# LSTM over gathered gate rows: each node tile's rows stay in a place of their own, and a gather fetches only the rows whose index changed

## The chip, the cores and the metric

The kernel runs on one core of a Trainium2 chip. The metric is the device time of one execution in microseconds; the median of several runs counts. The core has a matrix engine (TensorE, PE), a vector engine (VectorE, DVE), an activation engine (ScalarE, ACT), a general engine (GpSimd, POOL), a queue processor (SyncE, SP) and 16 DMA engines. Engines run their own instruction streams and wait for each other through semaphores.

## The reference

A graph of 6250 nodes has 106250 edges (50000 random ones in both directions, and a loop for each node), sorted by the receiver `dst`. Two layers run one after the other, each added to its input and normalised. The first is an LSTM over 17 neighbours of each node, where the "neighbours" are read from `dst`:

```python
col = edge_index[1]                       # = dst, which is sorted
seq = x[col].reshape(n, 17, 128)
# for each of the 17 steps, over all 6250 nodes:
gates = x_t @ w_ih.T + h @ w_hh.T + b     # 512 columns
i, f, g, o = split(gates, 4)
c = sigmoid(f) * c + sigmoid(i) * tanh(g)
h = sigmoid(o) * tanh(c)
x = layernorm(x + h_last @ w_lin.T + b_lin)
```

The second is an edge stage: for each edge a small MLP over 8 features gives weights, they are multiplied with 4 edge attributes and with the sender's row (gathered by `src`), and the messages are summed by `dst`, projected, added and normalised.

## The kernel before

Nodes stand in 49 tiles of 128 (6272 places, 22 of them padding), and the tiles in 13 chunks: 12 of 512 nodes and a last, narrow one of 128. The input part of the gates, x @ w_ih.T, depends on the node that is read and not on the step, so it is computed once for each node (`table_tile`, L330) and stored to the table `gates` in HBM, 2 KB a row. Step 0 gathers rows of x itself instead (L306), turns and multiplies them (`first_turn`, `first_gates`), so that it needn't wait for the table. Steps 1 to 16 are the list `WORK`, 208 pairs (step, chunk), in which index k counts.

For each k:

- POOL issues one indirect DMA for each of the chunk's tiles (L318). It takes 128 indices, a column of `seq_index`, and brings 128 rows of 2 KB from `gates`, one into each partition. They go to one of SLOTS = 5 slots (`rows[:, k % SLOTS]`); from the sixth on POOL first waits until the chunk 5 places back has been turned (`s_turned`, L314). Each gather has a semaphore of its slot, `s_wait[k % SLOTS]`.
- PE waits for the rows (L420). `turn_gate(k, q)` transposes the rows of gate q into a PSUM bank, 4 transposes for each gate and full chunk (L386), and `from_hidden(k, q)` adds the product with the hidden state, three matmuls of 512 columns, since weights and state are split in a high and a low part (L396). The order is turn 0, 1, 2, from_hidden 0, 1, 2, turn 3, from_hidden 3. Banks 0 to 3 belong to even k, 4 to 7 to odd k, so turn 0 waits for the DVE product two chunks back, turn 2 for the cell, turn 3 for `h_lo` (`s_hidden`).
- ACT applies sigmoid or tanh to the four gates (L562) and tanh to the cell of the chunk before (L529).
- DVE makes i*g (L728), the hidden product of the chunk before (L690), its high part (L695), f*c (L733), the low part (L700) and the sum (L738): six operations for each chunk. Nine further operations over 832 columns (`besides`, L648 to L682) prepare the edge stage, one behind each chunk from step 2 on.

SP loads the weights of the edge stage, x^T into `x1` and the attributes, 26 loads, one behind every second chunk from the start of WORK (L283 to L285). A factor is applied to a part of `w_out` on DVE in step 8 (L741). Behind the last step DVE's `residual(0)` (L783), the linear layer, the normalisation and the table of senders form a bridge (L436 to L800); POOL clears the sums in it (L325). The edge stage works in half groups of 4 edge tiles. POOL gathers 128 senders of 512 bytes for each tile (L862, 832 gathers), up to 4 half groups ahead of DVE's messages (L1040). ACT scales (L984), DVE multiplies (L1029 to L1040), PE runs the MLP (L877, L884, L896) and sums by receiver (L928).

SBUF holds `shared` (cell, the 5 slots and two candidates), beside `x1`, `attr`, `src_index` and others at places of their own.

Of the kernel before, what the change touches and what calls it, by code (L numbers as in the profile page):

```python
# [9 lines left out]
F32 = mybir.dt.float32  # L10
F32R = mybir.dt.float32r
I32 = mybir.dt.int32
# [26 lines left out]


# [16 lines left out]
RING = 4  # L57

# [40 lines left out]
def build(nc, t):  # L99
    ctx = ExitStack()  # L100
    with ctx:
# [10 lines left out]
        x1 = sb("x1", [P, NODE_TILES, DIM])  # L112
        dst = sb("dst", [P, EDGE_TILES])
        rel = sb("rel", [P, EDGE_TILES])
        base_row = sb("base_row", [P, EDGE_TILES])
        base_turn = sb("base_turn", [P, EDGE_TILES])
        iota = sb("iota", [P, P])
        src_index = sb("src_index", [P, EDGE_TILES], I32)
        attr = sb("attr", [P, 4, EDGE_TILES])
        ones = sb("ones", [P, 1])  # L120
        ident = sb("ident", [P, P])
        eps = sb("eps", [P, 1])
        w_up = sb("w_up", [P, P])
        a1 = sb("a1", [P, GROUP * P])
        a2 = sb("a2", [P, P])
        a3 = sb("a3", [P, P])
        b12 = sb("b12", [P, 2])
        w_out = sb("w_out", [P, MSG])
        w_lin = sb("w_lin", [P, P])
        b_lin = sb("b_lin", [P, 1])  # L130
        rounds_word = sb("rounds_word", [1, 1], I32)
        stats = sb("stats", [P, NODE_TILES, 6])
        moments = sb("moments", [P, NODE_TILES, 2])
        rstd = sb("rstd", [P, NODE_TILES])
        moments1 = sb("moments1", [P, NODE_TILES, 2])
        rstd1 = sb("rstd1", [P, NODE_TILES])


        slot_cols = 4 * 4 * HID
        pool_cols = SLOTS * slot_cols + 2 * CHUNK  # L140
        shared = sb("shared", [P, NODE_COLS + pool_cols])
        acc = shared[:, 0:NODE_TILES * MSG].rearrange("p (n f) -> p n f", f=MSG)
# [3 lines left out]
        s_wait = [sem(f"s_gather{i}") for i in range(SLOTS)]  # L146

        def flat_view(tile):
            return tile[:].rearrange("p a n -> p (a n)")

        def flat(tile, slot):
            return tile[:, slot].rearrange("p a n -> p (a n)")

        with ExitStack() as scope:

            cell = shared[:, 0:NODE_COLS]
            pool_of = shared[:, NODE_COLS:NODE_COLS + pool_cols]
            rows = pool_of[:, 0:SLOTS * slot_cols].rearrange("p (s j n) -> p s j n", s=SLOTS, j=4)
            candidate = pool_of[:, SLOTS * slot_cols:pool_cols].rearrange("p (s n) -> p s n", s=2)

            x_t = cell
            in_rows = pool_of[:, 0:8 * CHUNK].rearrange("p (s n) -> p s n", s=8)
            w_ih = pool_of[:, 8 * CHUNK:9 * CHUNK]

            seq_index = sb("seq_index", [P, NODE_TILES * STEPS], I32, scope=scope)
            not_below = sb("not_below", [P, EDGE_TILES], scope=scope)
            dst_int = not_below[:].bitcast(I32)
            mean_of = not_below[:, 0:P]
            count = sb("count", [P, 1], scope=scope)
            missed = sb("missed", [1, 1], scope=scope)  # L170
            bias2 = sb("bias2", [P, 8], scope=scope)
# [10 lines left out]
            up = sb("up", [P, 2, 4, P], scope=scope)  # L182
            inside = up[:].rearrange("p s j d -> p (s j d)")[:, 0:EDGE_TILES]

            s_wts, s_seq, s_idx, s_rest = sem("s_wts"), sem("s_seq"), sem("s_idx"), sem("s_rest")
            s_xt = [sem(f"s_xt{i}") for i in range(5)]
# [58 lines left out]

            def rows_in(c):
                return slice(FOURS[c][0], FOURS[c][-1] + 1)
# [10 lines left out]
            with nc.Block() as block:  # L258
                @block.sync
                def _(sp):  # L260
# [4 lines left out]
                    for tile, name in ((ident[:], "ident"), (bias2[:], "bias2"), (w_hh, "w_hh"), (w_lin[:], "w_lin")):  # L265
                        sp.dma_start(tile, t[name]).then_inc(s_idx, 16)
                    for n in range(NODE_TILES):
# [5 lines left out]
                    sp.dma_start(base_row[:], t["base_row"]).then_inc(s_const, 16)  # L273
                    sp.dma_start(base_turn[:], t["base_turn"]).then_inc(s_const, 16)
                    small = [(tile[:], t[name]) for tile, name in (
                        (src_index, "src"), (w_up, "w_up"), (a1, "a1"), (a2, "a2"),
                        (a3, "a3"), (b12, "b12"), (w_out, "w_out"), (b_lin, "b_lin"), (iota, "iota"))]
                    large = [(x1[:, tiles[0]:tiles[-1] + 1, :].rearrange("p a d -> p (a d)"),
                              t["x_t"][:, tiles[0] * P:(tiles[-1] + 1) * P]) for tiles in FOURS]
                    large += [(attr[:, k, :], t["attr4"][:, k * EDGE_TILES:(k + 1) * EDGE_TILES]) for k in range(4)]  # L280
                    loads = small + large
# [13 lines left out]
                def _(pool):  # L295
                    pool.memset(ones[:], 1.0)
                    pool.memset(eps[:], 1e-5).then_inc(s_set, 1)
                    pool.wait_ge(s_set, 1)
                    pool.wait_ge(s_seq, 16)
                    for c, (c0, width) in enumerate(CHUNKS):  # L300
# [4 lines left out]
                        for n in range(c0 // P, (c0 + width) // P):  # L305
                            pool.indirect_dma_start(  # L306
                                out=x1[:, n, :], out_offset=None, in_=t["x_rows"],
                                in_offset=bass.IndirectOffsetOnAxis(ap=seq_index[:, n * STEPS:n * STEPS + 1], axis=0),
                            ).then_inc(z_rows[c % SLOTS], 16)
# [15 lines left out]
                    pool.memset(shared[:, 0:NODE_TILES * MSG], 0.0).then_inc(s_zero, 1)  # L325
# [3 lines left out]
                def _(pe):  # L329
# [11 lines left out]
                    def first_turn(c):  # L341
# [11 lines left out]
                        for j in range(width // P):  # L353
                            last = pe.transpose(x_bank(c)[:, j * P:(j + 1) * P], x1[:, c0 // P + j, :], ident[:])
# [17 lines left out]
                    def turn_gate(k, q):  # L372
# [12 lines left out]
                        for j in range(CHUNKS[c][1] // P):  # L385
                            last = pe.matmul(bank[:, j * P:(j + 1) * P], rows[:, k % SLOTS, j, cols], ident[:],  # L386
# [25 lines left out]
                    landed = [0] * SLOTS  # L412
                    for k, (step, c) in enumerate(WORK):
                        c0, width = CHUNKS[c]
                        landed[k % SLOTS] += 16 * (width // P)
# [4 lines left out]
                        pe.wait_ge(s_wait[k % SLOTS], landed[k % SLOTS])  # L420
# [825 lines left out]
```

## Time and profile before

| | |
|---|---|
| median of 3 runs | 2174.67 us (2174.66 to 2175.22) |
| span of the profiled execution | 2710.9 us |
| PE, DVE, ACT, POOL busy in that span | 79%, 59%, 55%, 58% |
| granted TensorE clock, mean | 0.875 of full speed |
| moved by DMA | 299.97 MB, of it 263.36 MB by the software queue (the gathers) |

The page gives the span of the profiled execution, from its first to its last instruction, and no time for what lies around it. The span is 536 us longer than the median of the runs without a profile. Durations of single instructions are read from it; lengths of stages include what the profile adds. Times of instructions and idle times are in us, means of one instruction in ns. A releaser called "issue" means that nothing the profile shows held the engine back, "remote" that the releaser isn't known. Ends of matmuls are modelled. PE's clock has two levels, 1.2 and 2.4 GHz; the granted clock is the share of the upper one.

### The profile page before, as it was taken

What the parts mean: (1) busy time and instruction counts of PE and PEld (TensorE: products, weight loads), DVE (VectorE), ACT (ScalarE), POOL (GpSimd) and SP (SyncE); (2) the same over time, 40 slices, a digit from 0 to 9 for tenths busy, and PEclk for the clock granted to TensorE, in tenths of its full rate; (3) what the DMA queues carried; (4) which work ended last, traced back from release to release, by engine and by line L of the source; (5) the groups of instructions that cost most, each with busy time, mean ns of one, the idle gap of its engine ahead of it and who ended that gap; (6) DMA issues with size and microseconds to landing.
All of it is one profiled execution on the core that took longest, in us unless ns stands there. A gap on an engine that the chain in (4) does not pass through costs nothing.

```text
span 2710.9 us, 32629 instructions
## 1 busy us (share of the span) xinstructions
PE 2142.9 (79%) x10173; PEld 1641.3 (61%) x10173; DVE 1597.6 (59%) x3607; ACT 1490.2 (55%) x4706; POOL 1585.6 (58%) x1673
## 2 busy tenths in 40 slices
PE   6688888888888888888777777777778777877776
PEld 4567666776777767677555555555555555555554
DVE  4567566656666666666645545555555555555555
ACT  4545455445555555555366655656566656665655
POOL 5466666666666666665355555555556655655553
PEclk8899899899999999998778888778877888888888
DMA  6566666665665666565211111111111111112111
GB/s 236 170 195 183 193 206 188 181 173 171 178 180 170 181 173 180 170 178 152 67 40 46 45 41 44 43 41 45 45 39 47 46 41 46 47 40 75 41 42 41
DMA packets 118698, 299.97 MB, mean 111 GB/s; under 512 B 29058, under 2 KB 42604, under 8 KB 118524
## 3 DMA queue, kind: packets, MB, share of 16 engines
q0 software_dynamic: 90912, 263.36, 34.7%
q1 hardware_dynamic: 27612, 34.51, 3.8%
q8 instruction: 82, 1.34, 0.2%
q14 instruction: 92, 0.75, 0.1%
HBM read 278.50 MB, written 19.26 MB: 110 GB/s over the span
## 4 chain that ended last, share of the span: by engine, by line
ACT 21%; another core or an unknown queue 13%; PE 9%; issue 7%; DVE 1%; ACTq 0%; DVEq 0%
ACT bank L984 20%; PE bank L928 4%; PE bank L896 2%; PE bank L877 1%; PE bank L884 1%; ACT h L972 0%; ACT h L964 0%; PE bank L907 0%; PE bank L908 0%; DVE side L1029 0%; DVE msg L1032 0%; DVE msg L1030 0%; DVE y_high L1072 0%; PE bank L903 0%
## 5 line engine op out<-in xcount | busy, mean ns | idle before, releaser
L862 POOL DMA_INDIRECT sender<-table,src_index x832 | 784.8, 943 | 585.9 <-DVE msg L1040 303.3
L318 POOL DMA_INDIRECT shared<-gates,seq_index x784 | 742.1, 947 | 447.0 <-issue 207.6
L984 ACT ACTIVATE bank<-bank,attr 128x64 f32<-128x64 f32 x3328 | 702.2, 373 | 1.1 <-PE bank L896 0.5
L562 ACT ACTIVATE bank<-bank,bias 128x512 f32<-128x512 f32 (+1 forms) x624 | 375.7, 633 | 452.8 <-PE bank L396 329.2
L386 PE MATMUL bank<-ident,shared 128*128 128x128 f32 x3136 | 466.1, 292 | 173.3 <-DVE h_lo L700 135.0
L386 PEld LDWEIGHTS bank<-ident,shared 128*128 128x128 f32 x3136 | 396.9, 151 | 260.2 <-DVE h_lo L700 166.1
L928 PE MATMUL bank<-msg,select 128*128 128x256 f32 x1664 | 512.1, 453 | 1.2 <-DVE msg L1040 1.2
L1029 DVE TENSOR_TENSOR side<-sender,bank 128x192 f32<-128x192 f32 x416 | 146.6, 352 | 553.0 <-ACT bank L984 401.4
L896 PEld LDWEIGHTS bank<-a,h 64*128 64x128 f32 x1664 | 239.3, 219 | 349.6 <-issue 222.7
L896 PE MATMUL bank<-a,h 64*128 64x128 f32 x1664 | 282.6, 319 | 156.6 <-ACT bank L984 111.9
L928 PEld LDWEIGHTS bank<-msg,select 128*128 128x128 f32 x1664 | 349.0, 224 | 74.9 <-issue 7.4
L396 PE MATMUL bank<-h_hi,w_lo 128*128 128x512 f32 (+1 forms) x832 | 369.0, 443 | 1.1 <-issue 1.1
L728 DVE TENSOR_TENSOR shared<-bank,shared 128x512 f32<-128x512 f32 (+1 forms) x208 | 136.6, 657 | 393.6 <-ACT shared L562 205.8
L396 PE MATMUL bank<-h_hi,w_hi 128*128 128x512 f32 (+1 forms) x832 | 333.0, 400 | 0.0
L396 PE MATMUL bank<-h_lo,w_hi 128*128 128x512 f32 (+1 forms) x832 | 332.6, 400 | 0.3 <-issue 0.3
L964 ACT ACTIVATE h<-bank,b 128x512 f32<-128x512 f32 x104 | 74.1, 713 | 277.3 <-remote 185.0
L972 ACT ACTIVATE h<-bank,b 128x512 f32<-128x512 f32 x104 | 74.6, 717 | 256.5 <-remote 170.6
L877 PE MATMUL bank<-feats,a 128*128 128x512 f32 x208 | 128.8, 705 | 87.0 <-ACT h L972 60.8
L884 PE MATMUL bank<-h,a 128*128 128x512 f32 x208 | 130.0, 711 | 84.8 <-ACT h L964 78.1
L396 PEld LDWEIGHTS bank<-h_hi,w_hi 128*128 128x128 f32 x832 | 166.2, 200 | 34.7
L396 PEld LDWEIGHTS bank<-h_hi,w_lo 128*128 128x128 f32 x832 | 169.4, 204 | 19.6 <-issue 1.5
L396 PEld LDWEIGHTS bank<-h_lo,w_hi 128*128 128x128 f32 x832 | 168.7, 203 | 19.3 <-issue 1.3
(119 smaller groups left out, 2389.8 us busy)
## 6 DMA issues: line engine op xcount, KB each, us to landing
sender<-table,src_index POOLq DMA_INDIRECT x832
gates<-shared SPq DMA_DIRECT2D x49, 256.0 KB
shared<-gates,seq_index POOLq DMA_INDIRECT x784
feats<-attr_in SPq DMA_DIRECT2D x13, 256.0 KB
x<-x_t_in SPq DMA_DIRECT2D x12, 256.0 KB
table<-up SPq DMA_DIRECT2D x12, 256.0 KB, 2.3
out<-shared SPq DMA_DIRECT2D x9, 256.0 KB
shared<-x_t_in SPq DMA_DIRECT2D x3, 704.0 KB, 9.8
```

Source lines behind the costliest of these rows:

```text
L318: pool.indirect_dma_start(out=rows[:, k % SLOTS, j, :], out_offset=None, in_=t["gates"], in_offset=bass.IndirectOffsetOnAxis(ap=seq_index[ ...
L386: last = pe.matmul(bank[:, j * P:(j + 1) * P], rows[:, k % SLOTS, j, cols], ident[:], is_transpose=True, start=(j == 0), stop=False, skip_ ...
L396: last = pe.matmul(bank[:, 0:width], w[:, cols], h[:, c0:c0 + width], start=False, stop=(w is w_hi and h is h_hi), skip_group_check=True)
L562: act_e.activation(candidate[:, k % 2, 0:width] if gate == 2 else values, values, ACT.Tanh if gate == 2 else ACT.Sigmoid, bias=bias2[:, ga ...
L728: dve.tensor_tensor(added, put, added, ALU.mult).then_inc(s_ig, 1)
L862: pool.indirect_dma_start(out=sender[:, hg % 4, j, :], out_offset=None, in_=t["table"], in_offset=bass.IndirectOffsetOnAxis(ap=src_index[: ...
L877: pe.matmul(mlp_bank[:], a1[:, b * P:(b + 1) * P], feats[:, s % 2, :], start=True, stop=True).then_inc(e_p1, 1)
L884: pe.matmul(mlp_bank[:], a2[:], h1[:, g % 2, :], start=True, stop=True).then_inc(e_p2, 1)
L896: last = pe.matmul(weight_bank[hg % 2][:, j * P:(j + 1) * P], h2[channels, g % 2, j * P:(j + 1) * P], a3[channels, :], start=True, stop=True)
L928: last = pe.matmul(acc_bank[i % 2][:, 0:MSG], select[:, hg % RING, j, :], msg[:, hg % RING, j].rearrange("p k u -> p (k u)"), start=(tile ...
L984: last = act_e.activation(wy[:, j, :, k, :], w[:, 2 * i + j, :, min(k, 1), :], ACT.Copy, scale=attr[:, k, tile:tile + 1])
L1029: dve.tensor_tensor(along, row[:, :, 1:4, :], wy[:, :, 1, 1:4, :], ALU.mult).then_inc(e_side, 1)
```

## The change

All large buffers move into one SBUF tensor, `arena`, and share places over time. `rows` now has a place for each of the 49 node tiles (49 x 512 columns), which takes the room of `x1`, `attr`, `src_index`, `a1` to `a3`, `w_out`, `iota` and `acc` during the LSTM. A gather for (step, chunk) writes over the same tile's rows of the step before, so for step 2 and on it waits until that chunk was turned in the step before (13 places back), and in step 1 the last chunks wait until step 0's gates are done. Each chunk has a semaphore of its own.

At the start DVE makes a list `fetch` from `seq_index`: where a node's index of step t equals that of step t - 1 (t from 2 on), 65536 is added. The gathers use this list with a bound of 6271 and without an error beyond it, so a row with a larger index isn't fetched, and the place keeps the row of the step before. Step 0 and step 1 fetch all rows.

Since `x1` and the others now lie under `rows`, 23 of SP's loads move into the last step, each behind the transposes that free its place, and DVE scales `w_out` just ahead of `residual(0)`. `base_row` and `base_turn` share one buffer, so the second is loaded once the first has been used. The arithmetic is the same.

```diff
+SKIP = 1 << 16
...
+            rows = part(ROWS, NODE_TILES * ROW).rearrange("p (n g) -> p n g", g=ROW)
...
+            def last_row_end(end):
+                return before_last + ((end - ROWS - 1) // ROW) // 4 + 1
...
-                    for i, (tile, source) in enumerate(loads):
-                        sp.wait_ge(s_act, 8 * (i + 1))
+                    for tile, end, source in late:
+                        sp.wait_ge(s_turned, last_row_end(end))
                         sp.dma_start(tile, source).then_inc(s_rest, 16)
...
-                    pool.wait_ge(s_seq, 16)
+                    pool.memset(seq_same, 0.0).then_inc(s_fetch, 1)
+                    pool.wait_ge(s_fetch, 4)
...
                     for k, (step, c) in enumerate(WORK):
-                        if k >= SLOTS:
-                            pool.wait_ge(s_turned, k - SLOTS + 1)
                         c0, width = CHUNKS[c]
-                        for j in range(width // P):
-                            col = (c0 // P + j) * STEPS + step
+                        if step > 1:
+                            pool.wait_ge(s_turned, k - NCH + 1)
+                        elif ROWS + (c0 + width) // P * ROW > W_LIN:
+                            pool.wait_ge(z_gate, 3 * NCH)
+                        for n in range(c0 // P, (c0 + width) // P):
+                            col = n * STEPS + step
                             pool.indirect_dma_start(
-                                out=rows[:, k % SLOTS, j, :], out_offset=None, in_=t["gates"],
-                                in_offset=bass.IndirectOffsetOnAxis(ap=seq_index[:, col:col + 1], axis=0),
-                            ).then_inc(s_wait[k % SLOTS], 16)
+                                out=rows[:, n, :], out_offset=None, in_=t["gates"],
+                                in_offset=bass.IndirectOffsetOnAxis(ap=fetch[:, col:col + 1], axis=0),
+                                bounds_check=NODE_COLS - 1, oob_is_err=False,
+                            ).then_inc(s_wait[c], 16)
...
-                        pe.wait_ge(s_wait[k % SLOTS], landed[k % SLOTS])
+                        pe.wait_ge(s_wait[c], 16 * (width // P) * step)
...
+                    dve.wait_ge(s_seq, 16)
+                    dve.tensor_copy(seq_number, seq_index).then_inc(s_fetch, 1)
+                    dve.wait_ge(s_fetch, 2)
+                    dve.tensor_tensor(later, numbers[:, :, 2:STEPS], numbers[:, :, 1:STEPS - 1],
+                                      ALU.is_equal).then_inc(s_fetch, 1)
+                    dve.wait_ge(s_fetch, 3)
+                    dve.scalar_tensor_tensor(fetch[:], seq_same, float(SKIP), seq_number, ALU.mult,
+                                             ALU.add).then_inc(s_fetch, 1)
...
+                    scale_out()
                     residual(0)
```

## Rows read from the trace of the kernel before

**Rows 1.** Busy time of each engine by stretch; clock, DMA share and GB/s last
```profile
core 0: us, PE busy (x) PEld busy (x) DVE busy (x) ACT busy (x) POOL busy (x), PEclk, DMA share, GB/s
0.00:91.00 91.00, 62.37 (x252) 46.73 (x252) 47.81 (x71) 43.39 (x69) 48.01 (x55) 0.92 0.65 224
...
124.00:1296.00 1172.00, 997.24 (x5634) 838.21 (x5634) 756.75 (x1258) 599.58 (x1039) 723.37 (x765) 0.93 0.62 178
...
1339.00:2683.00 1344.00, 1022.08 (x3962) 706.57 (x3963) 723.46 (x2037) 809.97 (x3499) 784.79 (x832) 0.83 0.18 45
```
**Rows 2.** Groups by line, POOL: count, busy us, mean ns, idle before and releasers
```profile
L862 POOL DMA_INDIRECT sender<-table,src_index x832 | 784.8, 943 | 585.9 <-DVE msg L1040 303.3 <-issue 282.6
L318 POOL DMA_INDIRECT shared<-gates,seq_index x784 | 742.1, 947 | 447.0 <-issue 207.6 <-remote 152.6 <-PE bank L386 80.4
L306 POOL DMA_INDIRECT x<-x_rows_in,seq_index x49 | 47.7, 973 | 36.7 <-PE bank L337 20.6 <-issue 12.2 <-DMA seq_index<-seq_index_in 3.9
```
**Rows 3.** Timeline, POOL: start us, us, line; idle time before in brackets
```profile
91.59 0.94 POOL L318 DMA_INDIRECT shared<-gates,seq_index  x1 [6.31 <-DMA gates<-shared]
92.83 0.95 POOL L318 DMA_INDIRECT shared<-gates,seq_index  x1 [0.30 <-issue]
94.08 0.95 POOL L318 DMA_INDIRECT shared<-gates,seq_index  x1 [0.30 <-issue]
...
130.75 0.95 POOL L318 DMA_INDIRECT shared<-gates,seq_index  x1 [14.46 <-PE bank L386]
...
208.64 1.09 POOL L318 DMA_INDIRECT shared<-gates,seq_index  x1 [0.30 <-issue]
```
**Rows 4.** Timeline of PE, ACT and DVE, 697 to 710 us
```profile
697.06 1.47 PE L386 MATMUL bank<-ident,shared 128*128 128x128 f32 x12
...
698.84 0.40 PE L396 MATMUL bank<-h_hi,w_hi 128*128 128x512 f32 x1
...
701.60 1.47 PE L386 MATMUL bank<-ident,shared 128*128 128x128 f32 x12
...
703.60 0.66 ACT L562 ACTIVATE bank<-bank,bias 128x512 f32<-128x512 f32 x1 [5.67 <-remote]
...
705.51 0.69 DVE L690 TENSOR_TENSOR bank<-bank,tanh_c 128x512 f32<-128x512 f32 x1
...
708.17 0.66 PE L386 MATMUL bank<-ident,shared 128*128 128x128 f32 x4 [3.03 <-DVE h_lo L700]
...
709.42 0.70 DVE L690 TENSOR_TENSOR bank<-bank,tanh_c 128x512 f32<-128x512 f32 x1
```
**Rows 5.** Timeline: PE's last LSTM matmul, POOL's first and last edge gather
```profile
1295.73 0.28 PE L396 MATMUL bank<-h_hi,w_hi 128*128 128x128 f32 x1
...
1339.29 0.95 POOL L862 DMA_INDIRECT sender<-table,src_index  x1 [27.20 <-issue]
...
2681.82 0.94 POOL L862 DMA_INDIRECT sender<-table,src_index  x1 [0.30 <-issue]
```
**Rows 6.** Timeline of PE in the narrow chunk of the last step
```profile
1293.98 0.28 PE L396 MATMUL bank<-h_hi,w_lo 128*128 128x128 f32 x1
1294.09 0.28 PE L396 MATMUL bank<-h_lo,w_hi 128*128 128x128 f32 x1
1294.20 0.28 PE L396 MATMUL bank<-h_hi,w_hi 128*128 128x128 f32 x1
1295.39 0.33 PE L386 MATMUL bank<-ident,shared 128*128 128x128 f32 x1 [0.92 <-DVE h_lo L700]
```
**Rows 7.** Timeline of PE and ACT from the end of step 0 into step 1
```profile
97.06 0.50 PE L368 MATMUL bank<-first_hi,w_lo 128*128 128x512 f32 x1 [1.33 <-DVE h_lo L623]
...
104.96 0.60 ACT L513 ACTIVATE first_hi<-bank 128x512 fp32r<-128x512 f32 x1 [2.58 <-PE bank L354]
...
106.33 0.50 PE L368 MATMUL bank<-first_hi,w_lo 128*128 128x512 f32 x1 [2.72 <-issue]
...
121.99 0.47 PE L368 MATMUL bank<-first_hi,w_lo 128*128 128x128 f32 x1 [13.29 <-DVE first_lo L623]
...
123.97 2.78 PE L386 MATMUL bank<-ident,shared 128*128 128x128 f32 x12
```
**Rows 8.** Groups by line and shape, DVE operations over 832 columns
```profile
L654 DVE TENSOR_TENSOR rel<-dst,base_row 128x832 f32<-128x832 f32 x1 | 1.0, 1040 | 0.0
L662 DVE SCALAR_TENSOR_TENSOR up<-rel,not_below 128x832 f32<-128x832 f32 x1 | 1.0, 1017 | 0.0
...
L650 DVE CAST dst<-not_below 128x832 f32<-128x832 int32 x1 | 0.6, 583 | 0.0
```
**Rows 9.** DMA queues (packets, MB, share) and issues (KB each, us to landing)
```profile
q0 software_dynamic: 90912, 263.36, 34.7%
...
table<-up SPq DMA_DIRECT2D x12, 256.0 KB, 2.3
```

More of the change, by code:

```diff
@@ L38 @@
 SLOTS = 5
+SKIP = 1 << 16
+ROW = 4 * HID
+CELL = 0
+ROWS = CELL + NODE_COLS
+CAND = ROWS + NODE_TILES * ROW
+ARENA = CAND + 2 * CHUNK
+IN_ROWS = ROWS
+W_IH = IN_ROWS + 8 * ROW
+INDEX = W_IH + ROW
+X_ROWS = CAND - NODE_COLS
+W_LIN = X_ROWS - P
 GROUP = 8
@@ L57 @@
 RING = 4
+Y_LOW = 0
+X1 = ROWS
+ATTR = X1 + NODE_COLS
+SRC = ATTR + 4 * EDGE_TILES
+A1 = SRC + EDGE_TILES
+A2 = A1 + GROUP * P
+A3 = A2 + P
+W_OUT = A3 + P
+IOTA = W_OUT + MSG
+ACC = IOTA + P
+STATS = ACC + NODE_TILES * MSG
+MOMENTS = STATS + 6 * NODE_TILES
+RSTD = MOMENTS + 2 * NODE_TILES
+MOMENTS1 = Y_LOW + 36 * DIM
+RSTD1 = MOMENTS1 + 2 * NODE_TILES
+assert RSTD1 + NODE_TILES <= X1 and RSTD + NODE_TILES <= CAND
 def window_starts():
@@ L109, in sem, with part @@
             return ctx.enter_context(nc.semaphore(name))
-        x1 = sb("x1", [P, NODE_TILES, DIM])
+        arena = sb("arena", [P, ARENA])
+        def part(start, cols):
+            return arena[:, start:start + cols]
+        x1 = part(X1, NODE_COLS).rearrange("p (n d) -> p n d", d=DIM)
+        attr = part(ATTR, 4 * EDGE_TILES).rearrange("p (k n) -> p k n", k=4)
+        src_index = part(SRC, EDGE_TILES).bitcast(I32)
+        a1, a2, a3 = part(A1, GROUP * P), part(A2, P), part(A3, P)
+        w_out, iota = part(W_OUT, MSG), part(IOTA, P)
@@ L136, in build @@
[L136 to L142, printed above, removed]
+        rounds_word = small[0:1, 5:6].bitcast(I32)
         banks = [ps(f"bank{i}", [P, 512]) for i in range(8)]
         s_const = sem("s_const")
-        s_wait = [sem(f"s_gather{i}") for i in range(SLOTS)]
-        def flat_view(tile):
-            return tile[:].rearrange("p a n -> p (a n)")
@@ L151, in flat @@
-        def flat(tile, slot):
-            return tile[:, slot].rearrange("p a n -> p (a n)")
+        s_wait = [sem(f"s_gather{i}") for i in range(NCH)]
         with ExitStack() as scope:
[L156 to L159, printed above, removed]
+            cell = part(CELL, NODE_COLS)
+            rows = part(ROWS, NODE_TILES * ROW).rearrange("p (n g) -> p n g", g=ROW)
+            candidate = part(CAND, 2 * CHUNK).rearrange("p (s n) -> p s n", s=2)
@@ L385, in turn_gate @@
                         for j in range(CHUNKS[c][1] // P):
-                            last = pe.matmul(bank[:, j * P:(j + 1) * P], rows[:, k % SLOTS, j, cols], ident[:],
+                            last = pe.matmul(bank[:, j * P:(j + 1) * P], rows[:, CHUNKS[c][0] // P + j, cols], ident[:],
                                              is_transpose=True, start=(j == 0), stop=False,
@@ L484, in _ @@
                     pe.matmul(banks[5][:, P:2 * P], mean_of, w_up[:], start=True, stop=True)
-                    pe.matmul(banks[5][0:1, 0:1], count[:], ones[:], start=True, stop=True).then_inc(s_count, 1)
+                    pe.matmul(banks[5][0:1, 0:1], count, ones, start=True, stop=True).then_inc(s_count, 1)
                     for c in range(groups):
@@ L740, in _ @@
                             besides.pop(0)()
-                        if step == STEPS // 2 and c == 0:
-                            view = w_out[3 * MUL:P, P:2 * P]
-                            dve.wait_ge(s_rest, rest)
-                            dve.tensor_scalar(view, view, float(1 / np.sqrt(np.float32(3))), None, ALU.mult)
                     hidden_product(len(WORK) - 1)
@@ L781, in scale_projected, with scale_out @@
                             ALU.mult, ALU.mult).then_inc(s_up, 1)
+                    def scale_out():
+                        view = w_out[3 * MUL:P, P:2 * P]
+                        dve.wait_ge(s_rest, rest)
+                        dve.tensor_scalar(view, view, float(1 / np.sqrt(np.float32(3))), None, ALU.mult)
+                    scale_out()
                     residual(0)
@@ L883, in mlp2 @@
                         pe.wait_ge(e_h1, g + 1)
-                        pe.matmul(mlp_bank[:], a2[:], h1[:, g % 2, :], start=True, stop=True).then_inc(e_p2, 1)
+                        pe.matmul(mlp_bank[:], a2, h1[:, g % 2, :], start=True, stop=True).then_inc(e_p2, 1)
                     def mlp3(hg):
```

140 lines of the change are left out of this document (71 added, 69 removed).

## The prediction, made before the changed kernel was built or run

> **What bounds the kernel now.** I read the totals of the stages first, then the groups of the GpSimd queue (POOL), then single stretches in order of time. The span has two long stages: the LSTM steps 1 to 16 (124 to 1296 us) and the edge stage (1339 to 2683 us) [rows 1]. In the first, TensorE (PE) is busy 997 of 1172 us, VectorE (DVE) 757, ScalarE (ACT) 600, and the DMA engines 62%. None is full. POOL's busy time is little but the issuing of gathers: 784 gathers for the LSTM, 832 for the edges, 49 for step 0, about 945 ns each [rows 2]. Behind each comes a gap of 0.30 us that no other engine ends, so they start 1.25 us apart [rows 3]. That is 784 x 1.25 = 980 us in the LSTM and 832 x 1.25 = 1040 us in the edge stage, whatever the row size: a 512-byte row and a 2048-byte row cost the same 943 and 947 ns [rows 2].
>
> The profiled span is 2710.9 us, the median of the runs 2174.67 us; the page gives nothing of what lies around the span, so 536 us exist only under the profile. The trace shows where: from about 105 us on, ACT stands still every 12 us or so with its input ready. PE has finished the first gate's matmuls of a chunk at 699.2 us, ACT takes them at 703.60 after 5.67 us of idleness with an unknown releaser, and DVE and PE queue behind it (PE stops 3.03 us until h_lo is written at 708.1) [rows 4]. The first such hole ends at 104.96 us [rows 7]. So I don't take the stage lengths of the profile, but rebuild an undisturbed run from its durations.
>
> Ledger for an undisturbed run, POOL leading: first LSTM gather 91.6 us [rows 3]; + 980 = 1071.6; PE behind the last gathers + 7.3 (2.3 for a 256 KB transfer to land, as the table's store shows [rows 9], + 4.54 + 1.75 for the last two chunks, below, - 1.25 as the last full chunk's rows are issued one gather earlier) = 1079; to the first edge gather 43.3 (1296.0 to 1339.3) [rows 5]; + 1040; + 28.2 from POOL's last gather to the end (2682.8 to 2711) [rows 5]. Sum 2190, 16 us over the measured 2174.67. That closes within 0.7% with no free number, so I read the kernel as bound by POOL's issue rate in both stages.
>
> Ledger with PE leading in the LSTM: a full chunk of 512 nodes without a wait takes 4.54 us (transposes of one chunk at 697.06, of the next at 701.60) [rows 4]. A narrow chunk of 128 nodes takes 12 matmuls at 0.112 us and 4 transposes at about 0.1 us, 1.75 us; behind it PE waits 0.92 us for h_lo, and I put 0.75 us to it [rows 6]. A step is 12 x 4.54 + 1.75 + 0.75 = 57.0 us, 16 steps are 912 us. PE starts step 1 at 123.97 us, behind holes of 13.29 and 2.72 us caused by ACT, of which DVE's own chain would need some 1.3 [rows 7]; undisturbed that is about 109.3 us. So PE could be done at 109.3 + 912 = 1021 us, and the total would be 2132 us, 43 us under the measured time. The first ledger is the nearer.
>
> **The change, part by part.**
> - Rows fetched. dst is sorted and a node's 17 indices are consecutive, so almost all of a node's steps have the same index. Counted from the inputs, 5,522 of the 94,080 rows of steps 2 to 16 change, 7.5 of 128 in a gather; step 1 fetches all. The instructions stay 784. What falls for certain are bytes of the software queue's 263 MB [rows 9]: 784 x 256 KB, 205 MB, become some 24 MB. They are worth nothing by themselves: the DMA engines are at 62% [rows 1].
> - POOL's price of a gather. No row shows a gather with fewer rows. From below: if the 945 ns go with the rows fetched, 7.5/128 of them, 0.06 us, and the gap of 0.30 remain, 0.36 us. From above: the slowest LSTM gather in the stretch I read took 1.09 us, 0.14 more, so 1.39 us with the gap [rows 3]. The 128 indices must still be read and compared. I take a price nearer the lower end, since for 94% of the rows no transfer has to be made up. The exact value doesn't matter: POOL ends before PE as soon as 91.6 + 784 p + 7.3 is under 1021, at p below 1.176 us, 8% off the 945 ns. Then PE leads, and the stage ends at 1021 instead of 1079: **-58 us**.
> - The rule of the Trainium skill that bears on this: DMA: Bandwidth & Descriptors, section SWDGE vs HWDGE vs iDMA, says that software on the GpSimd cores computes one descriptor pair for each DMA operation. By that rule the price follows the rows not skipped, 0.36 us, and the total is the same 2117 us, with PE leading by far. By the trace (no dependence on bytes) the price could as well be one of the instruction, and the total 2174 us. The rows here can't decide between these.
> - A place for each node tile instead of a ring of 5 chunks. A gather of step t waits for the transposes of its own chunk in step t-1, 13 chunks back instead of 5. In the profile POOL stands 14.46 us at 116 us for the first slot (its row of 130.75) [rows 3], but undisturbed PE would have turned that chunk at about 115 us, so I count 0 (if the hole were real, 14 us of gain). It also lets POOL run ahead of ACT's holes, which helps the profile alone.
> - Start. POOL and DVE first make the list: a cast of 833 columns 0.58, a compare 1.04, a multiply-add 1.02 us, by the same operations on 832 columns [rows 8]. DVE's w_hi begins some 2 us after 4.54 and low(0) is ready at 7.7 instead of 7.64. The cover is ACT's h_hi, which is on the path anyway. POOL's first step-0 gather moves by 2.7 us; it waits for PE later. 0 us; without the cover 2.7.
> - Loads moved into the last step: 23 of them, 6.2 MB, each after the transposes that free its place; the last place is free once chunk 5 of 13 is turned, 25 us into the step, so 32 us remain. At the 224 GB/s of the first stretch [rows 1] all 6.2 MB take 28 us, and most begin earlier. Hidden, 0 us. Behind them are queued DVE's scaling of w_out and then residual(0), and PE's mean matmul, so if they are late the bridge moves by the lateness, up to about 5 us. The scaling itself adds one 128-column operation, 0.3 us at most.
> - Whether DVE and ACT keep up with PE: DVE's product comes every 3.91 us when it is not waiting (705.51 to 709.42) [rows 4], under 4.54. It is next, with 14% to spare.
>
> Sum: 2174.67 - 58 = **2117 us**. Against the profiled span the same edit is worth less or more, depending on what becomes of ACT's holes; I forecast only the runs.
>
> **The rivals.**
> 1. The price stays. If the 945 ns belong to the instruction (all 128 indices read and compared, vectors of fixed length), POOL leads as before and only the byte count falls: 2174 us, 2168 to 2179. The same results if the change doesn't do what it says (the rows beyond the bound are fetched from somewhere), or if the missing 43 us of the second ledger lie in the edge stage and PE already leads the LSTM. For it: equal times for both row sizes. Against: the ledger that closes.
> 2. The price rises: slower. With a bound given, each gather may carry another register instruction, or take a slower loop. POOL is the bound, so all 784 pay in full; from +0.006 us each it is over 0.2%. Between 0 and the +0.14 us above I take +0.05: 784 x 0.05 = 39, 2214 us. Against it: 94% of the rows leave work out.
> 3. Only part: a price between 1.176 and 1.24 us, or PE meets waits I don't see (narrow chunks, h_lo) and loses 5 to 40 us of the 58: 2125 to 2165 us.
>
> **How the numbers follow.** Forecast 0.52 (2117; own range 2095 to 2135: PE's wait at the narrow chunk 0 to 1.5 us a step is +-12, the two ledgers' distance of 16 and 43 us lets the gain be 43 to 74). Rival 1: 0.22, of which 0.17 within 0.2%. Rival 2: 0.20. Rival 3: 0.06. Faster 0.52 + 0.06 + 0.05 = 0.63, same 0.17, slower 0.20; 0.2% (4.3 us) is about what a measurement of this kernel can tell from no change. The range runs from 2095 over rival 3 and rival 1 to 2200, and leaves out most of rival 2 and a little below.
>
> **What would show it.** In the profile after: the start-to-start time of the LSTM gathers in steps 2 to 16, well under 1.176 us for the forecast, 1.25 for rival 1, above for rival 2; in step 1, with all rows fetched, 1.25 or more. POOL should wait for PE's transposes through the whole LSTM, PE should have no wait that ends with a landing, and its clock should stay at the upper level. The software queue's 263 MB should fall to some 82 MB. The last loads should land before the last chunk. Edge gathers unchanged at 1.25 us. The prediction fails if the compare costs as much as a descriptor, or if PE doesn't reach 4.54 us a chunk in undisturbed runs.

## The result, and the profile after

The changed kernel takes 2212.76 us (median of 4 runs, 2212.12 to 2214.28), the kernel before 2174.66 us (4 runs, 2171.55 to 2175.22): ratio 1.018, 95% interval 1.0168 to 1.0193, 38.1 us slower. The forecast was 2117 us, faster. What came is rival 2, whose sum was 2214 us.

One thing must be known to read the traces. The profiled execution of the changed kernel spans 2211.7 us in a run of 2213.39 us, and the other three runs took 2212.12 to 2214.28 us, so a profile adds nothing. The profile of before (2710.9 us) looks like the profiles of four chips met below, on which the median of the kernel before was 2700 to 2775 us and the profiled run was no longer than the rest (e1: 2694.33 us among runs of 2682.09 to 2727.99). I read it as taken on such a chip; its chip isn't on record. I call a chip "plain" if the kernel before takes about 2175 us there, and "halting" if it takes 2700 to 2775 us. A ratio is always against runs of the kernel before on the same chip.

The page of the changed kernel: its span, its DMA packets, the software queue (packets, MB, share of 16 engines), and the shares of the chain that ended last by engine.

```profile
span 2211.7 us, 33416 instructions
...
DMA packets 118704, 119.01 MB, mean 54 GB/s; under 512 B 70886, under 2 KB 84432, under 8 KB 118524
...
q0 software_dynamic: 90912, 82.35, 15.5%
...
POOL 35%; issue 11%; PE 1%; DVE 0%; DMA 0%; ACT 0%; POOLq 0%; SPq 0%; DVEq 0%
```

The page before has, for all queues together:

```profile
DMA packets 118698, 299.97 MB, mean 111 GB/s; under 512 B 29058, under 2 KB 42604, under 8 KB 118524
```

The bytes fell as planned, from 263.36 to 82.35 MB, but the queue's packet count is the same 90912 as before [rows 9]: skipped rows still leave their packets, small ones (70886 are now under 512 bytes, 29058 were before). The chain that ended last is POOL's edge gathers and the gaps behind them; it begins at 1150 us, behind the LSTM, so of the LSTM it says nothing; there POOL's idle time has to. POOL's groups of the changed kernel, times busy and idle in us, mean in ns:

```profile
L908 POOL DMA_INDIRECT sender<-table,arena x832 | 785.3, 944 | 280.8 <-issue 279.3 <-DVE msg L1086 1.5
L351 POOL DMA_INDIRECT arena<-gates,fetch x784 | 785.2, 1001 | 244.6 <-issue 233.3 <-DMA gates<-arena 5.9 <-PE bank L420 5.5
L337 POOL DMA_INDIRECT arena<-x_rows_in,fetch x49 | 48.6, 992 | 20.6 <-issue 12.8 <-DVE fetch L744 5.0 <-PE bank L371 2.5
```

Against [rows 2], the edge gathers, which weren't changed, kept their price (943 and 944 ns); the LSTM gathers went from 947 to 1001 ns. POOL waits 5.5 us for PE's transposes in all, and not through the whole LSTM. Gathers of the changed kernel one by one, in step 1, where every row is fetched, and in the middle of the stage, where 7.5 of 128 are (start, duration, what ended the idle time before):

```profile
79.41 1.00 POOL L351 DMA_INDIRECT arena<-gates,fetch  x1 [0.31 <-issue]
80.71 0.99 POOL L351 DMA_INDIRECT arena<-gates,fetch  x1 [0.30 <-issue]
82.01 1.00 POOL L351 DMA_INDIRECT arena<-gates,fetch  x1 [0.30 <-issue]
...
707.58 1.00 POOL L351 DMA_INDIRECT arena<-gates,fetch  x1 [0.31 <-issue]
708.89 1.00 POOL L351 DMA_INDIRECT arena<-gates,fetch  x1 [0.30 <-issue]
710.19 1.00 POOL L351 DMA_INDIRECT arena<-gates,fetch  x1 [0.30 <-issue]
```

They start 1.303 us apart in both places, where [rows 3] had 1.25: a gather with the bound is the longer one even where it skips nothing. 784 x 0.052 is 41 us, and the result is +38.1. The groups of PE's waits (total us, times, longest), the weight loads of the same transposes, which run ahead of them, and the busy time of the LSTM show who is late:

```profile
PE bank L420 <- DMA arena<-gates,fetch: 63.3, 131, 1.3
PE bank L420 <- DVE h_lo L733: 15.0, 16, 0.9
```

```profile
L420 PEld LDWEIGHTS bank<-ident,arena 128*128 128x128 f32 x3136 | 355.0, 141 | 174.1 <-DMA arena<-gates,fetch 125.2
```

```profile
core 0: us, PE busy (x) PEld busy (x) DVE busy (x) ACT busy (x) POOL busy (x), PEclk, DMA share, GB/s
110.00:1103.00 993.00, 915.00 (x5544) 755.47 (x5543) 743.90 (x1237) 604.65 (x1021) 759.80 (x760) 1.00 0.12 26
```

PE waits for landings 131 times (63.3 us; its weight loads 125.2 us), and the DMA engines are busy 12% of the stage: what PE waits for are gathers not yet issued, not rows on their way. The granted clock is 1.00 here, PE's upper level, so the clock cost nothing.

### The profile page after: what moved, and what is told of

The parts are those of the page before. It is cut to its first block and busy times, and to the rows that moved or that the text cites. A ratio compares the mean times of both kernels' runs of the same rounds, so it can differ in the third digit from the quotient of the medians.

```text
span 2211.7 us, 33416 instructions
## 1 busy us (share of the span) xinstructions
PE 1911.1 (86%) x10173; PEld 1475.6 (67%) x10173; DVE 1582.1 (72%) x3610; ACT 1513.0 (68%) x4706; POOL 1631.0 (74%) x1674
## 2 busy tenths in 40 slices
DMA packets 118704, 119.01 MB, mean 54 GB/s; under 512 B 70886, under 2 KB 84432, under 8 KB 118524
## 3 DMA queue, kind: packets, MB, share of 16 engines
q0 software_dynamic: 90912, 82.35, 15.5%
## 5 line engine op out<-in xcount | busy, mean ns | idle before, releaser
L908 POOL DMA_INDIRECT sender<-table,arena x832 | 785.3, 944 | 280.8 <-issue 279.3
L351 POOL DMA_INDIRECT arena<-gates,fetch x784 | 785.2, 1001 | 244.6 <-issue 233.3
L1030 ACT ACTIVATE bank<-bank,arena 128x64 f32<-128x64 f32 x3328 | 697.3, 337 | 178.6 <-DVE msg L1078 175.7
L594 ACT ACTIVATE bank<-bank,small 128x512 f32<-128x512 f32 (+1 forms) x624 | 393.6, 634 | 366.4 <-PE bank L430 355.8
L420 PE MATMUL bank<-ident,arena 128*128 128x128 f32 x3136 | 419.5, 275 | 78.9 <-DMA arena<-gates,fetch 63.3
L420 PEld LDWEIGHTS bank<-ident,arena 128*128 128x128 f32 x3136 | 355.0, 141 | 174.1 <-DMA arena<-gates,fetch 125.2
L942 PEld LDWEIGHTS bank<-arena,h 64*128 64x128 f32 x1664 | 205.1, 191 | 335.1 <-issue 183.2
L942 PE MATMUL bank<-arena,h 64*128 64x128 f32 x1664 | 242.8, 287 | 163.5 <-ACT bank L1030 162.0
L1076 DVE TENSOR_TENSOR msg<-sender,bank 128x256 f32<-128x256 f32 x416 | 171.5, 412 | 0.0
L1078 DVE TENSOR_TENSOR msg<-sender,bank 128x192 f32<-128x192 f32 x416 | 143.7, 345 | 0.0
```

Of the source, the lines that this page charges most:

```text
L351: pool.indirect_dma_start(out=rows[:, n, :], out_offset=None, in_=t["gates"], in_offset=bass.IndirectOffsetOnAxis(ap=fetch[:, col:col + 1] ...
L420: last = pe.matmul(bank[:, j * P:(j + 1) * P], rows[:, CHUNKS[c][0] // P + j, cols], ident[:], is_transpose=True, start=(j == 0), stop=Fal ...
L594: act_e.activation(candidate[:, k % 2, 0:width] if gate == 2 else values, values, ACT.Tanh if gate == 2 else ACT.Sigmoid, bias=bias2[:, ga ...
L908: pool.indirect_dma_start(out=sender[:, hg % 4, j, :], out_offset=None, in_=t["table"], in_offset=bass.IndirectOffsetOnAxis(ap=src_index[: ...
L942: last = pe.matmul(weight_bank[hg % 2][:, j * P:(j + 1) * P], h2[channels, g % 2, j * P:(j + 1) * P], a3[channels, :], start=True, stop=True)
L1030: last = act_e.activation(wy[:, j, :, k, :], w[:, 2 * i + j, :, min(k, 1), :], ACT.Copy, scale=attr[:, k, tile:tile + 1])
```

## The experiments

My theory after the result: the bound itself makes a gather's instruction 0.05 us longer, whatever it skips. The rivals: the list of skipped rows costs (time per row compared or skipped); the writes into a large arena cost; the extra instruction of each bounded gather costs.

**Bound and skipping apart.** e1 takes the bound away and fetches all rows into the places:

```diff
-                                bounds_check=NODE_COLS - 1, oob_is_err=False,
...
-                    dve.scalar_tensor_tensor(fetch[:], seq_same, float(SKIP), seq_number, ALU.mult,
+                    dve.scalar_tensor_tensor(fetch[:], seq_same, 0.0, seq_number, ALU.mult,
```

> The changed kernel with the bound and the list's additions taken out: places for all tiles stay, every gather fetches all 128 rows (263 MB again). Theory B (the bound given with the instruction adds 52 ns to each LSTM gather, and POOL's queue sets the time): LSTM gathers 945 ns, 1.25 us apart, total 2213 - 784 x 0.052 = 2172 us. Rival P (the price comes from the new places or from the index list's place): 1.30 us apart, 2213 us. Rival S (the skipping costs): 2172 us as well.

e2 has only the second of these edits: the bound stands, and no index is beyond it.

> The changed kernel with the bound kept, but no index ever beyond it: all rows are fetched, 263 MB. Theory B: gathers 1000 ns, 1.30 us apart, 2213 us, so the 181 MB that the change saves are worth nothing. Rival S (rows that are skipped cost more than rows that are fetched): 945 ns, 2172 us. A rival in which skipping already gives something back: above 1000 ns and above 2213 us.

e3 is the kernel before with the bound:

```diff
                                 in_offset=bass.IndirectOffsetOnAxis(ap=seq_index[:, col:col + 1], axis=0),
+                                bounds_check=NODE_COLS - 1, oob_is_err=False,
```

> The kernel before, ring of 5 slots, with nothing but the bound given to its LSTM gathers; no index lies beyond it. Theory B: 2175 + 784 x 0.052 = 2215 us. Rivals P and S: 2175 us, no change.

e7 puts all indices from step 2 on beyond the bound, so the steps compute with the rows of step 1:

```diff
-                    pool.memset(seq_same, 0.0).then_inc(s_fetch, 1)
+                    pool.memset(seq_same, 1.0).then_inc(s_fetch, 1)
...
-                    dve.tensor_tensor(later, numbers[:, :, 2:STEPS], numbers[:, :, 1:STEPS - 1],
-                                      ALU.is_equal).then_inc(s_fetch, 1)
+                    dve.tensor_scalar(seq_same.rearrange("p (n t) -> p n t", t=STEPS)[:, :, 0:2],
+                                      numbers[:, :, 0:2], 0.0, None, ALU.mult).then_inc(s_fetch, 1)
```

> The changed kernel with every index of steps 2 to 16 beyond the bound, so these gathers fetch nothing (their steps use the rows of step 1, which changes what is computed). Theory B: the price doesn't depend on how many of the 128 rows are skipped, 1000 ns, 2213 us. The forecast's reason (the price goes with the rows fetched): if 7.5 of 128 rows had left most of the price in place by some fixed part, 0 rows should still be lower than 7.5; in the pure form 0.30 us apart and PE leading, 2117 us.

All four ran on a halting chip. POOL's LSTM gathers in e1, e2, e3 and e7, in this order:

```profile
L351 POOL DMA_INDIRECT arena<-gates,fetch x784 | 744.3, 949 | 406.5 <-issue 210.1 <-remote 156.9 <-PE bank L419 33.2
```
```profile
L351 POOL DMA_INDIRECT arena<-gates,fetch x784 | 786.6, 1003 | 400.0 <-issue 212.7 <-remote 143.3 <-PE bank L420 37.2
```
```profile
L318 POOL DMA_INDIRECT shared<-gates,seq_index x784 | 785.9, 1002 | 430.3 <-issue 209.5 <-remote 128.7 <-PE bank L387 85.2
```
```profile
L351 POOL DMA_INDIRECT arena<-gates,fetch x784 | 783.7, 1000 | 405.2 <-issue 213.6 <-remote 134.1 <-PE bank L420 50.7
```

Without the bound 949 ns, with it 1003 (128 rows fetched), 1002 (in the kernel before, ring of 5 and no arena) and 1000 ns (none fetched from step 2 on). The rows skipped don't count, nor do the places. The times say little here, since POOL also waits for others (33 to 85 us for PE, 129 to 157 for an unknown releaser): e1 2696.38 us, ratio 0.9971 (0.9935 to 1.0007); e2 2733.34, 1.0109 (1.0037 to 1.018); e3 2722.39, 1.007 (1.0036 to 1.0104); e7 2730.81, 1.0121 (1.0051 to 1.0191).

**Repeats, and the extra instruction.** The counts of instructions are 33416 with the bound and 32632 without (after, e1): one more for each of the 784 gathers. e9 makes the register with the bound once, ahead of the loop:

```diff
+                    bound = pool.to_reg(NODE_COLS - 1)
                     for k, (step, c) in enumerate(WORK):
...
-                                bounds_check=NODE_COLS - 1, oob_is_err=False,
+                                bounds_check=bound, oob_is_err=False,
```

It ran with f1, f2 and f3, which are e1, e2 and e3 again.

> The changed kernel, complete, but the bound's value is put into a register once, ahead of the LSTM gathers, and all 784 use that register; in the changed kernel each gather has its own register instruction ahead of it (33416 instructions against 32632 without a bound). Theory R (the 52 ns are that extra instruction): gathers start 1.25 us apart, 2172 us. Theory U (they belong to the gather with a bound itself, whose own record grew from 945 to 1000 ns while the gap stayed 0.30): 1.30 us apart, 2213 us.

> The same kernel as e1_places_no_bound (places kept, no bound, all rows fetched), again, since the chip of that run executed even the kernel before in 2702 us. There its gathers already took 949 ns. Theory B: 2213 - 784 x 0.052 = 2172 us. Rival P: 2213 us. Against the kernel before (2175) the new places, the moved loads and the list at the start are then worth under 5 us together.

> The same kernel as e2_bound_all_rows (places, bound, all rows fetched, 263 MB), again. Theory B: 2213 us, the time of the changed kernel, so 181 MB less are worth nothing. Rival: the smaller traffic of the changed kernel gives back a part, then this one is above 2213 us.

> The same kernel as e3_before_with_bound (ring of 5 slots, only the bound added), again. Theory B: 2175 + 41 = 2216 us. Rival P: 2175 us.

The chip halted too. e9's page and its gathers:

```profile
span 2691.9 us, 32633 instructions
```
```profile
L352 POOL DMA_INDIRECT arena<-gates,fetch x784 | 783.3, 999 | 385.3 <-issue 212.3 <-remote 118.8 <-PE bank L421 47.4
```

783 instructions are gone and the gather still takes 999 ns, with starts 1.30 us apart. The extra instruction isn't what spaces the gathers out; the bounded gather itself is longer. (e9's edit met no plain chip, so no time shows this, only the gathers.) f1 947 ns, f2 1002, f3 999. Times: f1 2696.61, ratio 0.9983 (0.9944 to 1.0023); f2 2733.11, 1.011 (1.0017 to 1.0203); f3 2711.49, 1.0034 (0.9986 to 1.0081); e9 2716.76, 1.0047 (1.0002 to 1.0093).

**How far POOL leads.** On a plain chip I then took gathers away. e4 leaves out all of step 2 and on:

```diff
                     for k, (step, c) in enumerate(WORK):
+                        if step > 1:
+                            continue
...
-                        pe.wait_ge(s_wait[c], 16 * (width // P) * step)
+                        pe.wait_ge(s_wait[c], 16 * (width // P))
```

> The changed kernel without any LSTM gather from step 2 on; PE works on the rows of step 1 in all steps, so the result is another, and POOL is out of the way. This measures the second leg of the forecast, PE leading: 57.0 us a step, LSTM end 58 us earlier than with POOL at 1.25 us, total 2117 us by the ledger (2213 - 41 - 58 = 2114). If PE meets waits that the trace didn't show, it comes out higher, and the forecast would have missed even with a cheap gather.

e6 leaves out 3 of 49 gathers in each of these steps, e6b 12 of 49 (the wait's count follows):

```diff
                         for n in range(c0 // P, (c0 + width) // P):
+                            if step > 1 and c % 4 == 3 and n % 4 == 3:   # e6
+                            if step > 1 and n % 4 == 3:                  # e6b
+                                continue
```

> The changed kernel with 46 of 49 gathers a step from step 2 on (the last tile of chunks 3, 7 and 11 keeps the rows of step 1, so its numbers are others). POOL needs 46 x 1.303 = 59.9 us a step, PE 57.0: POOL still leads, each of the 45 gathers left out gives its full 1.303 us: 2213 - 58.6 = 2154 us. If POOL's queue isn't what sets the LSTM's time, less.

> The changed kernel with 37 of 49 gathers a step from step 2 on (one tile of each full chunk keeps the rows of step 1). POOL needs 48.2 us a step, PE 57.0: PE leads, the same time as without gathers, about 2117 us. If POOL led to the end it would be 2213 - 180 x 1.303 = 1978 us.

e8 gathers for 64 of the 128 partitions:

```diff
+                            parts_of = P if step == 1 else P // 2
...
-                                out=rows[:, n, :], out_offset=None, in_=t["gates"],
-                                in_offset=bass.IndirectOffsetOnAxis(ap=fetch[:, col:col + 1], axis=0),
+                                out=rows[0:parts_of, n, :], out_offset=None, in_=t["gates"],
+                                in_offset=bass.IndirectOffsetOnAxis(ap=fetch[0:parts_of, col:col + 1], axis=0),
```

> The changed kernel with gathers over 64 partitions from step 2 on (the other 64 keep the rows of step 1). It measures how the price goes with the rows an instruction handles, fetched or not. If POOL makes up an entry for each of them, skipped or not: about half of the part that goes with rows is gone, well under 1000 ns, and PE may lead (about 2117 us). If the 1000 ns belong to the instruction: 2213 us.

The kernel before took 2175.53 us here (11 runs).

| | us | ratio (95%) | LSTM gathers, mean ns |
|---|---|---|---|
| e4, 49 of 784 gathers | 2117.94 | 0.9738 (0.9722 to 0.9754) | 1001 |
| e6, 739 | 2156.64 | 0.9914 (0.9898 to 0.9931) | 1002 |
| e6b, 604 | 2119.87 | 0.9741 (0.9725 to 0.9757) | 1001 |
| e8, 784 over 64 partitions | 2169.99 | 0.9976 (0.9965 to 0.9987) | 945 |

e6 leaves out 45 gathers and saves 56.1 us against the changed kernel's 2212.76 us, measured apart from it, beside a kernel before of 2174.66 us. That is 1.25 us for each, near the full 1.303: POOL leads. e6b leaves out 180, which would be 235 us, but stops where e4 does. ACT's gate groups of the changed kernel in the middle of the stage, and of e4, show the pace (start, duration, idle before):

```profile
699.27 0.66 ACT L594 ACTIVATE bank<-bank,small 128x512 f32<-128x512 f32 x1 [2.01 <-PE bank L430]
...
704.60 0.66 ACT L594 ACTIVATE bank<-bank,small 128x512 f32<-128x512 f32 x1 [2.15 <-PE bank L430]
...
709.76 0.66 ACT L594 ACTIVATE bank<-bank,small 128x512 f32<-128x512 f32 x1 [1.99 <-PE bank L430]
```
```profile
699.94 0.66 ACT L596 ACTIVATE bank<-bank,small 128x512 f32<-128x512 f32 x1 [1.35 <-PE bank L432]
...
704.46 0.66 ACT L596 ACTIVATE bank<-bank,small 128x512 f32<-128x512 f32 x1 [1.35 <-PE bank L432]
...
708.99 0.66 ACT L596 ACTIVATE bank<-bank,small 128x512 f32<-128x512 f32 x1 [1.35 <-PE bank L432]
```

A chunk takes 5.2 us in the changed kernel, four gathers of 1.303, and 4.53 us without gathers, PE's own pace. The last matmul of the hidden state in e4, and in e6b POOL's waits:

```profile
1013.42 0.28 PE L432 MATMUL bank<-h_hi,w_hi 128*128 128x128 f32 x1
```
```profile
POOL arena L353 <- issue: 145.2, 463, 1.5
POOL arena L353 <- PE bank L422: 131.4, 140, 2.5
```

In e6b POOL waits for PE 140 times, as the forecast wanted it of the change. e8's gathers one by one:

```profile
700.23 0.94 POOL L352 DMA_INDIRECT arena<-gates,fetch  x1 [0.31 <-issue]
701.47 0.94 POOL L352 DMA_INDIRECT arena<-gates,fetch  x1 [0.30 <-issue]
702.72 0.94 POOL L352 DMA_INDIRECT arena<-gates,fetch  x1 [0.30 <-issue]
```

64 rows fewer make a gather 0.06 us shorter, under 1 ns a row. By a straight line through these two sizes, an estimate, some 0.88 us of a bounded gather don't depend on rows.

**The rest of the change, in time.** Next came e1's edit against the kernel before again. g1, g3, g7 and g9 (the edits of e1, e3, e7, e9) fell on a halting chip (before 2775.18 us):

> Places kept, no bound, all rows fetched (as e1_places_no_bound), on a chip that runs the kernel before in 2175 us, if it is one. Theory B (the bound costs 55 ns a gather, whatever rows it skips, and POOL leads): 2213 - 784 x 0.052 = 2172 us.

> The kernel before with only the bound added (as e3_before_with_bound). Theory B: 2175 + 784 x 0.052 = 2216 us, and so the whole loss of the change comes from this one argument.

> All rows of steps 2 to 16 skipped (as e7_all_rows_skipped; the steps use the rows of step 1, which changes what is computed). Its gathers took 1000 ns, as with 7.5 rows fetched and with all 128. Theory B: 2213 us, the time of the changed kernel.

> The changed kernel with the bound's value in one register for all gathers (as e9_bound_register). There the instruction count fell by 783 and the gathers still took 999 ns, 1.30 us apart. Theory U (the price belongs to the bound, not to the extra register instruction): 2213 us. Theory R: 2172 us.

g1 2759.52, ratio 0.9952 (0.9919 to 0.9984); g3 2787.81, 1.0052 (1.0016 to 1.0087); g7 2795.74, 1.0074 (1.004 to 1.0107); g9 2755.65, 0.9948 (0.9918 to 0.9979). Where POOL doesn't lead, these differences of half a per cent have no clear owner: g9 with the bound is as fast as g1 without, and I draw nothing from them on the bound. One of them stays unexplained: g9, with the bound in one register, is 40 us faster than g7, with a register instruction for each gather, at the same spacing of gathers (1001 and 1004 ns). The two differ in the skipped rows as well, and no run separates this. Last, h1 (e1's edit) and h3 (e3's):

> The changed kernel without the bound, all rows fetched, on a chip that runs the kernel before in 2175 us, if it is one. Theory B: 2213 - 784 x 0.052 = 2172 us. A rival that puts the loss on the places or the moved loads: 2213 us.

> The kernel before with only the bound added, on a chip that runs the kernel before in 2175 us, if it is one. Theory B: 2175 + 784 x 0.052 = 2216 us. Any rival that puts the loss on the places, the moved loads or the skipped rows: 2175 us.

h1 met a plain chip: 2174.26 us (10 runs) against 2174.00 (13 runs), ratio 1.0004 (0.9994 to 1.0013). h3 met a halting one: 2714.44, 1.0038 (0.9998 to 1.0079). h1's gathers, POOL's timeline in the stage, and the stage's busy time:

```profile
L351 POOL DMA_INDIRECT arena<-gates,fetch x784 | 743.1, 948 | 243.9 <-issue 237.3 <-DMA gates<-arena 5.4 <-PE bank L419 1.2
```
```profile
699.60 0.95 POOL L351 DMA_INDIRECT arena<-gates,fetch  x1 [0.30 <-issue]
700.86 0.94 POOL L351 DMA_INDIRECT arena<-gates,fetch  x1 [0.30 <-issue]
702.10 0.94 POOL L351 DMA_INDIRECT arena<-gates,fetch  x1 [0.30 <-issue]
```
```profile
110.00:1060.00 950.00, 901.77 (x5508) 754.75 (x5507) 737.87 (x1228) 601.39 (x1017) 717.76 (x758) 1.00 0.75 217
```

So the changed kernel without its bound and its skipping is the kernel before in time. What the change adds besides these two (the places, the 13-chunk distance, the list, the late loads) sums to nothing that shows, and the 181 MB are worth nothing either: h1 moves 217 GB/s with the DMA engines 75% busy, the changed kernel 26 GB/s at 12%, and the gathers' spacing is the shorter one in h1. Bound and skipping together are the 38 us. That it is the bound and not the skipping is shown by the gathers: step 1 of the changed kernel skips nothing and has the long ones on a plain chip, and so have e2, e3 and their repeats on halting ones.

Why 38 and not 41 us? POOL's first and last LSTM gather and its first edge gather, in the changed kernel and in h1:

```profile
76.79 1.01 POOL L351 DMA_INDIRECT arena<-gates,fetch  x1 [5.89 <-DMA gates<-arena]
...
1099.70 1.00 POOL L351 DMA_INDIRECT arena<-gates,fetch  x1 [0.30 <-issue]
...
1151.26 0.96 POOL L908 DMA_INDIRECT sender<-table,arena  x1 [26.31 <-issue]
```
```profile
76.47 0.94 POOL L351 DMA_INDIRECT arena<-gates,fetch  x1 [5.36 <-DMA gates<-arena]
...
1057.12 0.95 POOL L351 DMA_INDIRECT arena<-gates,fetch  x1 [0.30 <-issue]
...
1111.65 0.95 POOL L907 DMA_INDIRECT sender<-table,arena  x1 [26.82 <-issue]
```

From the first to the last LSTM gather the changed kernel needs 42.3 us more (1022.9 against 980.6). Of this, 3.0 us come back on the way to the first edge gather (51.6 against 54.5) and 1.0 us behind it, and the start is 0.3 us later: 38.6 us, the difference of the two spans.

## Why the prediction was wrong

- **The ledger with POOL leading held**, though its ground was partly wrong. It took the 536 us between the profile's span and the runs for something that exists only under the profile. The run behind the changed profile is 1.7 us longer than its span, and the changed profile has no such holes; e1's, on a halting chip, has them. The rebuild could come near because durations and gaps of POOL are alike on both kinds of chip (947 to 949 ns). Held against h1, which has the time of the kernel before, it is right in the two long terms (980 against 981.6 us, 1040 against 1039.8), and its surplus of some 17 us over h1's span is in the start (91.6 against 76.5) and the end (28.2 against 21.6), less 3.0 us by which the stretch between the stages is longer in h1 (50.6 against 53.6) and the 1.6 us of the first term. POOL led: e6 shows 1.25 us of time for each gather taken away.
- **The ledger with PE leading held as well.** Forecast: PE could be done at 1021 us and the total be 2132, or 2117 from the measured median. e4 ends the LSTM at 1013.7 us, 4.53 us a chunk against 4.54, with the 0.93 us wait at the narrow chunk [rows 6], and takes 2117.94; e6b takes 2119.87. That the end is so near 1021 is in part luck: PE's transposes of step 1 begin at 96.7 us in e4 and not at 109.3, and the 16 steps take 917 us and not 912. The gain of 58 us was there to be had. The threshold of 1.176 itself wasn't tested: for each of the 49 tiles of a step e6b's 37 gathers come to 0.98 us, and PE leads; e6's 46 come to 1.22 us, and POOL leads.
- **The step that failed is POOL's price of a gather.** The bounds were 0.36 and 1.39 us, and I took a value near the lower one, "since for 94% of the rows no transfer has to be made up". Measured: 1.303, over the threshold of 1.176 and over the 1.25 of before. Time per row is under 1 ns of it (e8), and e2, e7 and the changed kernel show the same 1000 to 1003 ns for 128, 0 and 7.5 rows fetched. The nearest row was against my choice and stood in [rows 2]: a four times larger row cost 4 ns. I noted that and read it as "bytes are free" only; it also says that the price isn't the transfers'.
- By the rule of the Trainium skill (DMA: Bandwidth & Descriptors, section SWDGE vs HWDGE vs iDMA), software on the GpSimd cores computes one descriptor pair for each DMA operation. That each fetched row is such an operation and that the price goes with their number was my reading, not the page's words. The runs speak against it: the queue has 90912 packets whether 128, 7.5 or 0 rows of a gather are fetched, and the gather takes 1000 to 1003 ns.
- **Rival 2** was right in size (+0.05 assumed, +0.052 measured) and half right in its mechanism: the extra register instruction exists (784 more) but isn't what spaces the gathers out; the bounded gather itself is longer (e9). Its chance of 0.20 was too small, because "94% of the rows leave work out" was counted against it without a row that shows the price falling with rows. **Rival 1** had the reason right (the price is the instruction's) and missed the bound's own 0.05 us.
- **The places, the start, the late loads: 0 us together**, as predicted, by h1 (its interval is -1.3 to +2.8 us); one by one they weren't measured. The loads are issued by 1076.7 us (SP's last in the changed kernel), under the last gathers of the LSTM, which end at about 1100. That the 14.46 us hole of [rows 3] was not there to gain follows from the same equal times; no profile of the kernel before from a plain chip shows it.
- **DVE keeps up**, as predicted: e4 and e6b run at PE's pace.
- The range ended at 2200 and left out rival 2's 2214, which is where the time was.

What stays open: the time of the kernel before with the bound added was measured only where POOL doesn't lead (e3, f3, g3, h3: 1.0034 to 1.007); that it would be 38 us on a plain chip is argued from its 1000 ns gathers and from h1 and the change, not shown. What inside the bounded gather takes the 54 ns isn't shown either. On a plain chip no version measured computes all rows and beats the kernel before; the 58 us behind POOL would want fewer gathers, for instance none for tiles whose 128 indices all stay the same, which was not tried.

## What to carry over

Before an edit makes a queue's instructions "do less", find in the trace whether their price follows the amount at all: two groups of the same operation with different sizes answer it, and if they cost the same, only fewer instructions help. When such an instruction's queue sets the time, an option on it is paid in full for each instance, here 784 times 0.05 us. And a span far from the median may come from another chip and not from the profiler: rebuild the run from single durations, and doubt the reason for the difference until a second profile shows it.

## What was not expected of the hardware

- An indirect gather costs POOL 0.94 to 0.95 us and a gap of 0.30 us, nearly all fixed: half the rows save 0.06 us (e8); a bound adds 0.054 us (947 to 1001 ns); skipped rows leave their packets (90912 in e2, in the changed kernel and in e7).
- Chips differ. On halting ones ACT stands about 4 us every 12 us or so in the LSTM (in one place of [rows 4] plainly with its input ready), the granted clock is 0.86 to 0.88 on average against 0.98, and the kernel before takes 2700 to 2775 us against 2175. POOL's gathers last as long on both, and so do ACT's gate operations over 512 columns (658 ns in e1, 659 in h1); ACT's 64-column scalings of the edge stage don't (372 against 337 ns). What halts ACT no run here shows. Each chip was met once, so that it is the chip and not something of the moment isn't shown either.
